# Three of a block's four x products and three of its four x transposes move in between the one-hot products

## The reference

```python
msg = jnp.concatenate([x[src], edge_attr], axis=1) @ W1 + b1       # (50000, 128)
agg = jax.ops.segment_sum(msg, dst, num_segments=100000)           # (100000, 128)
y   = jnp.concatenate([x, agg], axis=1) @ W2 + b2                  # (100000, 64)
out = layernorm(x + y)
```

## Time and profile before

| | |
|---|---|
| median of 3 executions | 1043.76 us (1041.74 to 1046.48) |
| the profiled execution | 1046.84 us |
| its span, first to last instruction | 1045.0 us |
| mean granted TensorE clock in it | 0.760 |
| TensorE matmul busy (PE) | 667.1 us, 64% |
| TensorE weight load busy (PEld) | 599.9 us, 57% |
| VectorE, ScalarE, GpSimd busy | 413.0, 445.3, 395.9 us |

### The profile page before, as it was taken

One profiled execution on the slowest core, in us unless ns is written; L12 is line 12 of the kernel. 1 busy time (PEld: TensorE's weight loads), 2 busy tenths in 40 slices (PEclk: granted clock), 3 DMA queues, 4 the chain that ended last, 5 costly groups with the idle time before them and its releaser, 6 DMA issues.

```text
span 1045.0 us, 25986 instructions
## 1 busy us (share of the span) xinstructions
PE 667.1 (64%) x8086; PEld 599.9 (57%) x8087; DVE 413.0 (40%) x945; ACT 445.3 (43%) x2113; POOL 395.9 (38%) x422
## 2 busy tenths in 40 slices
PE   2346676577577657657666657765765765678764
PEld 1234565466466556546556557654664755568753
DVE  3465343333333534333443323533333433247543
ACT  0012355345346535534544535553453543366422
POOL 6735334433533443443443443344244343521000
PEclk9997677678778877876877867876786786688766
DMA  2112223223323422322332322332233232233101
GB/s 54 29 25 49 56 65 86 70 65 82 73 66 90 100 60 65 95 61 65 86 77 59 93 62 65 96 87 69 65 81 73 69 94 60 45 96 79 55 22 41
DMA packets 171918, 71.39 MB, mean 68 GB/s; under 512 B 64737, under 2 KB 165615, under 8 KB 171888
## 3 DMA queue, kind: packets, MB, share of 16 engines
q1 hardware_dynamic: 107728, 51.75, 17.1%
q0 software_dynamic: 12544, 12.87, 6.6%
q10 hardware_dynamic: 51616, 6.41, 3.9%
HBM read 45.37 MB, written 25.60 MB: 68 GB/s over the span
## 4 chain that ended last, share of the span: by engine, by line
PE 60%; issue 32%; another core or an unknown queue 3%; DVE 2%; POOL 1%; DVEq 1%; ACT 0%; DMA 0%; ACTq 0%; POOLq 0%
PE ps_y L538 26%; PE ps_y L529 13%; PE ps_z L463 8%; PE ps_x L518 6%; PE ps_t L455 4%; PE ps_y L575 1%; PE ps_y L556 1%; PE ps_x L596 1%; DVE onehot_x L947 0%; DVEq L947 0%; PE ps_y L596 0%; DVE z_rest L792 0%; DMA feat<-in_x,src_idx 0%; DVE z L901 0%
## 5 line engine op out<-in xcount | busy, mean ns | idle before, releaser
L430 POOL DMA_INDIRECT feat<-in_x,src_idx x392 | 387.3, 988 | 547.8 <-PE ps_t L455 422.8
L538 PE MATMUL ps_y<-z_window,onehot 128*128 128x64 bf16 x5292 | 290.4, 211 | 283.6 <-issue 281.4
L538 PEld LDWEIGHTS ps_y<-z_window,onehot 128*128 128x128 bf16 x5292 | 238.9, 110 | 334.6 <-issue 326.6
L658 ACT ACTIVATE square<-ps_y 128x64 bf16<-128x64 f32 x784 | 161.9, 238 | 403.8 <-PE ps_y L529 401.7
L917 DVE TENSOR_TENSOR onehot<-node_of_col,dst_in_group 128x2304 bf16<-128x2304 bf16 x98 | 133.2, 1360 | 329.1 <-PE ps_y L529 308.1
L529 PE MATMUL ps_y<-wx,x_t 128*128 128x128 f32 x784 | 155.0, 359 | 6.8 <-issue 6.8
L658 ACT ACTIVATION_READ_ACCUMULATOR square<-ps_y 128x1 f32 x784 | 159.2, 224 | 0.0
L529 PEld LDWEIGHTS ps_y<-wx,x_t 128*128 128x128 f32 x784 | 134.4, 258 | 8.8 <-issue 8.3
L463 PE MATMUL ps_z<-wz,feat_t 97*128 97x64 f32 x784 | 102.4, 288 | 6.8 <-issue 5.4
L463 PEld LDWEIGHTS ps_z<-wz,feat_t 97*128 97x128 f32 x784 | 100.0, 207 | 8.6 <-issue 8.2
L623 ACT ACTIVATE feat_t<-ps_t 97x512 f32<-97x512 f32 x98 | 53.8, 591 | 112.3 <-remote 83.1
(11 more groups left out here) (148 smaller groups left out, 239.6 us busy)
## 6 DMA issues: line engine op xcount, KB each, us to landing
xin<-in_x SPq DMA_DIRECT2D x97, 192.0 KB
out<-yout SPq DMA_DIRECT2D x97, 192.0 KB
xin<-in_x SPq DMA_DIRECT2D x99, 64.0 KB
out<-yout SPq DMA_DIRECT2D x99, 64.0 KB
feat<-in_x,src_idx POOLq DMA_INDIRECT x392
feat<-in_edge_attr ACTq DMA_DIRECT2D x97, 64.0 KB
z<-in_src SPq DMA_DIRECT2D x1, 192.0 KB
z<-in_dst SPq DMA_DIRECT2D x1, 192.0 KB
```

Of the source, the lines that this page charges most:

```text
L430: nc.gpsimd.indirect_dma_start(out=feat[h][:, feat_at(k) + c, 0:C], out_offset=None, in_=x[:, :], in_offset=bass.IndirectOffsetOnAxis(ap=s ...
L538: nc.tensor.matmul(ps_y[h][:, col:col + C], onehot[h][:, slot, a, :], z_window[h][:, slot, part * C:(part + 1) * C], start=False, stop=Fal ...
L658: sq = nc.scalar.activation(square[:, q, :], ps_y[h][:, q * C:(q + 1) * C], ACT.Square, accum_out=sumsq[:, h, q:q + 1])
```

## The change

In each `block_sum` a helper `between(n)` runs after each of the 18 groups of three one-hot products. After every third group, so after every nine products, it puts one float32 operation: x products 0, 1, 2 and then transposes 0, 1, 2. The fourth x product and the fourth transpose stay at the end. The waits for x_t and for the loaded x now stand ahead of the first one-hot product, and `hots_used` is counted up by the last of the 54 products instead of the first x product, so ahead of the further products.

```diff
             def turn_x(k, h):
 
                 pe.wait_ge(x_loaded[h], 16 * transfers(k + 1, h))
                 wait_rounds(pe, x_ready[h], k)
-                for g in range(G):
-                    tr = nc.tensor.transpose(ps_x[h][:, g * P:(g + 1) * P], xin[h][:, g, :], ident[:, :])
-                tr.then_inc(x_used[h], 1)
+                for g in range(G - 1):
+                    transpose_x(h, g)
+                transpose_x(h, G - 1).then_inc(x_used[h], 1)
...
+                def between(n):
+
+                    if n % 3 == 2 and n // 3 < G - 1:
+                        dense(n // 3)
+                    elif n % 3 == 2:
+                        transpose_x(h, n // 3 - (G - 1))
...
                             for part in range(3):
-                                nc.tensor.matmul(ps_y[h][:, col:col + C], onehot[h][:, slot, a, :],
-                                                 z_window[h][:, slot, part * C:(part + 1) * C], start=False, stop=False, skip_group_check=True)
+                                mm = nc.tensor.matmul(ps_y[h][:, col:col + C], onehot[h][:, slot, a, :],
+                                                      z_window[h][:, slot, part * C:(part + 1) * C], start=False, stop=False, skip_group_check=True)
+                            if slot * A + a == SLOTS * A - 1:
+                                mm.then_inc(hots_used[h], 1)
+                            between(slot * A + a)
 
                 pe.wait_ge(hot_ready, b + 1)
+                pe.wait_ge(x_ready[h], k + 1)
+                pe.wait_ge(x_loaded[h], 16 * transfers(k + 2, h))
...
-                pe.wait_ge(x_ready[h], k + 1)
-                dense(0).then_inc(hots_used[h], 1)
-                for g in range(1, G - 1):
-                    dense(g)
                 dense(G - 1).then_inc(y_done[h], 1)
-                turn_x(k + 1, h)
+
+                transpose_x(h, G - 1).then_inc(x_used[h], 1)
```

More of the change, by code:

```diff
@@ L512, in _, with transpose_x @@
             nc.tensor.transpose(ps_a[0:PAIRS, 0:P], lacking[:, :], ident[:, :]).then_inc(s_units_t, 1)
+            def transpose_x(h, g):
+                return nc.tensor.transpose(ps_x[h][:, g * P:(g + 1) * P], xin[h][:, g, :], ident[:, :])
             def turn_x(k, h):
```

## The result

The changed kernel takes 1072.2 us (median of 4 runs, 1069.93 to 1075.64) where the kernel before took 1043.12 (4 runs, 1041.74 to 1046.48): a ratio of 1.0269 [1.0242, 1.0296], slower. The profiled execution has a span of 1071.9 us against 1045.0, at a mean granted clock of 0.748 against 0.760. The sum of the prediction met the time; several of its terms did not hold.

The account below looks back on a forecast made before the run. One TensorE program, starved during gathers, was taken to set the time. 41 rounds at +0.47 give +19, plain blocks +4, last blocks +5: +28 us on 1046.8, or 1072 on the median of 1043.8; range 1036 to 1093.

Parts of the forecast that it names:

- (A): Whole kernel: passages between bf16 and float32 work cost more than the starving hides; 1053 to 1092 us, chance 0.57.
- What gets out ahead of the starving: Block 0's first run: 28 records out, 2.79 us left instead of 3.06; 0.27 saved, 0.20 kept a round.
- my end of 2.11: Block 0 behind the starving: if records count, 35 go out first and 2.11 us of work are left.
- keep its length and 12 records: Block 0: the starving of TensorE during gathers was to stay at 9.1 us and 12 records.
- the later head of block 0: Start of block 0: one instruction more was to cost 0.1 us a round (0 to 0.1).
- Five passages in block 1, 0.57: Block 1: five more bf16-to-float32 passages, about two at low clock, cost 0.57 us a round (0.45 to 0.75).
- Behind block 1: no term: Between blocks: the head of block 1 was to cost nothing; no idle time behind block 1 was priced.
- The clock: Behind the starving: with the rise at the same moment, work saved at 1.2 GHz counts at half its time there.
- rival B: Behind the starving: the clock rises later, 3.5 us later costing 1.7 a round; 1085 to 1140 us, chance 0.11.
- the mark against B: Whole run: mean granted clock stays within 0.02 of 0.76; a larger fall would show that the clock rises later.
- The tail: Last five blocks, with loops paced by DVE: +5 us (0 to +9), including up to 1 us for a late x load.
- the eight plain blocks' +4: Eight blocks without starving or long waits: passages cost 0.45 us each, +4 us in all.

Follow-up runs that it names:

- the block-0 kernel: Products and transposes put in between in block 0 only, block 1 in its old order, against the kernel before: 1031.39 us, 0.9749.
- the two halves of the change: Against the kernel before, the changed order in block 0 only, 0.9749, and in block 1 only, 1.0159.

## Why the prediction was right, and which of its steps were not

The time was right, 1072 against 1072.2, and so was the place of the loss: in the rounds of the table block 1 pays more than the starving saves. The mechanism of the forecast (A), that passages cost more than the starving hides, was not: the passages cost 0.32 a round and the starving gave back 0.48, so that by these two alone the change would have been a gain. What turns it into a loss is the gap behind block 1, for which the prediction had no term, and the later rise of the clock. That the sum met the time is luck. The terms came out so:

- **What gets out ahead of the starving.** I took 28 records, between 21 and 35. It is 35: what counts is records. The first run now lasts 1.98 us instead of 1.0, and 33 to 37 records went out in every kernel of the table. What is left takes 2.10 us, my end of 2.11, and not 2.79; but it is 22.4 records with cheap passages ahead of transposes, where that end had 19 with dear ones. Saved are 0.97 at the low clock, 0.48 at the full-clock price, where I had 0.27 and counted 0.20. The starving itself changed as well: its end stays with the gathers, 11.4 us behind the first one in both kernels, so it became shorter; it also passed fewer records in a microsecond, 8.6 in all instead of 13.3. I had it keep its length and 12 records. Since its end is tied to the gathers, the later head of block 0, for which I counted 0.10, costs nothing.
- **Five passages in block 1, 0.57.** They are cheaper: 0.08 ahead of an x product, but 0.035 ahead of a transpose, 0.32 in all at full clock. At the low clock, in the round shown, an x product of two records takes 517.99 - 517.42 = 0.57, where two transposes would take 0.43: 0.14, as forecast. Of block 1, 3.78 of 5.72 us ran at the low clock in that round, where it was 1.49 of 3.67, because it starts sooner.
- **Behind block 1: no term.** This is what the prediction lacked. It had 0.10 for the head of block 0 and "nothing for block 1, whose head is handled while the one before still runs". Block 1's own head did cost nothing at the low clock (516.92 follows 516.71 directly), but the gap of 0.43 (0.52 from start to start) ahead of the transposes of gathered chunks opened behind block 1, and 0.17 to 0.67 ahead of blocks at full clock.
- **The clock.** "As long as the rise comes at the same moment": it came 0.47 us later on average, give or take 0.2, which is 0.24 us a round. That is rival B at about a seventh of the delay I had put in. I wrote that the clock would decide if it rose 3.5 us later; it decided without that, for with the rise of the block-0 kernel (4.35) the changed kernel would pay 0.49 less in a round and roughly break even. The mean granted clock, 0.748 against 0.760, stayed within the 0.02 that I had set as the mark against B; as a mark it was too coarse, for the four runs of the changed kernel alone lie between 0.747 and 0.768.
- **The tail.** I counted +5 for the last five blocks, with up to 1 us, once, for a late x load. From the start of block 84 to the last product it is 142.3 instead of 130.8 us, +11.5, with some of the eight plain blocks' +4 in it. The waits for x loads at the head take 4.4 of that in two blocks. The worse of them on the timeline, and in the chain that ended last:

```profile
1003.58 0.66 PE L548 MATMUL ps_y<-z_window,onehot 128*128 128x64 bf16 x9 [3.28 <-DMA xin<-in_x]
```

```profile
997.00 0.70 DVE yout L971
...
999.14 1.04 SPq L348
...
1000.76 2.69 DMA xin<-in_x
```

  SP issues the loads only behind the stores of a block (yout, L343 and L348), and all 54 one-hot products now stand behind the last load. I had read the queue rightly, but priced the lateness by the issue alone; the 2.69 us of the transfer come on top.

On the pages: the Trainium skill ("TensorE: Matmul & The Clock Gate", Step-by-step: what each phase is for) has the queue pull weight loads ahead of products in flight. The trace agrees in part: a passage to a transpose is nearly hidden, 0.035 us, one to an x product is not, 0.08. The Trainium skill (same page, Part 4: PE-mode transpose) says that a transpose doesn't count as busy for the clock in the same way. No run here tells that apart: with the transposes together at the end the low clock still lasted 4.82 us a round, with them spread out and the waits at their use 4.93, on another chip of the same kind.

So the total was right because errors cancel. In a round I had -0.20 + 0.57 + 0.10 = +0.47; measured is -0.48 for what is left behind the starving, +0.32 for the passages, +0.52 for the gap and +0.24 for the clock, +0.60, against 0.55 from the table. Over the whole run errors cancel a second time. I had +19 and +4 us for the rounds and +5 for the last blocks; by the starts of block 0 the rounds grew by 16.4, what stands behind them by 12.5, and what stands ahead of them, for which I had nothing, shrank by 2.0.

What stays open: why some chips starve TensorE during gathers and others don't; what starves it; why a gap opens behind a block with insertions though six records stand at its end, and also behind one without insertions and with two records; why fewer records pass in the starving of every changed kernel; why the two halves of the change, each of which shortens the low stretch, do not do so together; and how much of the change the waits at its heads cost in the common rounds.

## What to carry to other kernels

When an engine is starved at a fixed number of records, try to put the dearest records of its queue under the starving, in one group, and nothing in between anywhere else: on one chip that kernel gained 3.2%, where the one with insertions in both blocks (and its waits at their use) lost 1.7%. Count passages between bf16 and float32 work, but also ask what the engine's sequencer has to do behind a block, and price a moved wait by the whole transfer behind it. And try the halves of a change apart: here their effects did not add, and the low clock's stretch is where they did not.

## What the runs showed of the hardware

- The same kernel, before the change, took 1043 to 1060 us in three of the comparisons and 651 to 652 in two, by the chip. In the former TensorE gets one or two records in 0.7 or 1.4 us, from the moment that some 35 records of a block are out until 2.4 us behind the last gather of the round; in the latter there is no trace of it beneath gathers that go out at the same pace. Without gathers it takes 617.6 us on a chip of the first kind.
- A change of the order that is worth 3.2% on a chip of one kind (0.9683) costs 0.75% on one of the other (1.0075). A comparison has to be made on one chip, and says nothing of the other kind.
- Under the starving a float32 record costs no more than a bf16 one, one or two in 0.7 or 1.4 us for either, against 0.11 and 0.03 us a record outside of it.
- Behind the last one-hot product of a block 12 float32 records in one run leave no gap to the next instruction (1.44 us from that product to it at full clock). With two, four or six float32 records there instead, TensorE stands idle for 0.58, 0.49 and 0.58 us in the rounds shown.
